# Graph layer edge loop: four PSUM banks for edge products with three pairs ahead, three banks for sums

## The chip, the cores and the metric

The kernel runs on one core of one Trainium2 chip. The metric is the device time of one execution in microseconds (us). The kernel before takes 6811.75 us, the median of three runs (6805.44 to 6826.25). The profiled execution is a fourth one, of 6786.33 us.

## The reference: what is computed

The program is a graph attention layer, a mixture of experts, a five-layer graph convolution and a second mixture, each with a residual add. The change touches the graph convolution alone. On 3125 nodes of 256 features and 53,125 edges (sorted by destination) with 128 features each, every layer `l` computes:

```
xl   = h @ W[l] + b[l]
ee   = edge_attr @ We[l] + be[l]
msg  = norm * relu(xl[row] + ee)
agg  = zeros_like(xl).at[col].add(msg)
conv = agg + relu(xl + root[l]) / deg
h    = h + (relu of, except in the last layer) batch_norm(conv)
```

All of it is in float32.

## The kernel before, in words

`graph_layers` loops over the five layers. In each, `graph_layer_inputs` makes the table `xl_table` in DRAM, `graph_layer_edges` runs the edge loop, and `graph_layer_norm` normalises. The change is in `graph_layer_edges`, with two small edits in `constants` and in `lagging_bases`.

The edges are padded to 416 tiles of 128. The edge loop has 26 iterations (`ITERS`) of 16 tiles (`BODY`), and an iteration works in eight pairs of tiles; `u` is the pair's number in its iteration, 0 to 7. So a layer has 208 pairs and the five layers have 1040. Every engine has its own instruction stream, and they meet only at semaphores. For a pair the work is:

- POOL (L1730) gathers the 128 source rows of each tile by an indirect DMA, two gathers a pair, into a buffer `g` of 16 tiles. The gather of a pair of the next iteration waits (L1745 to L1747) until DVE and ACT have used the same slots in this one.
- SP (L1705, L1708) loads the gather's indices and the edge features `ea`, in two halves of eight tiles. A half of `ea` is loaded again when its four product pairs are done (`used`, L1716).
- PE `products` (L1761) multiplies edge features by `We`, two tiles into one PSUM bank of `ep`. Two banks (`EB = 2`) are used in turn, and the wait at L1758 holds the products of a pair until DVE has read the pair two before. They are issued two pairs ahead of the sums.
- DVE `add_pair` (L1849) adds the gathered rows to the products and writes `msg`. It waits for the products, the two gathers, and the sums that last read this slot of `msg`.
- ACT (L1833) applies the relu to `msg`. DVE (L1854) makes the scaled one-hot matrix of the even tile, ACT (L1815, L1818) that of the odd tile.
- PE `sums` (L1774) multiplies messages by one-hot matrices into one PSUM bank of `ps`. Four banks are used in turn (`SB = 8` tiles), so the wait at L1769 is for the pair four before to have been added.
- DVE `add_sums` (L1862) adds a tile's sums to its window of `agg`, at an address that a register holds. It runs `LAG = 4` tiles behind, so at pair `u` DVE adds the sums of pair `u - 2`.

At pair `u` the order on PE is: products of `u + 2`, sums of `u`, and at `u = 1` also `node_tile` (L1783), the root term of one node tile. On DVE it is: `add_pair(u)`, `add_sums(u - 2)` of the even tile, the one-hot matrix, `add_sums(u - 2)` of the odd tile; at `u = 0` it also loads 16 window addresses into registers, and at `u = 6` and 7 it adds the node tile. On ACT it is: one-hot matrix of the odd tile, at `u = 3` the relu of the node tile (L1829, which waits for `node_tile`), then the relu of pair `u`.

A matmul of this source is recorded as two, so the profile has eight matmuls for the sums of a pair and four for its products.

Of the kernel before, what the change touches and what calls it, by code (L numbers as in the profile page):

```python
# [24 lines left out]
P = 128  # L25
# [14 lines left out]
GROW = HROW + HEADS  # L40
ACC = NP + P
LAG = 4
LAYERS = 5
XROW = D + 2
PARTS = 3
# [20 lines left out]
class Kernel:  # L66


    def __init__(self, nc, a, ctx):
        self.nc, self.a, self.ctx = nc, a, ctx  # L70
        self.sems, self.live = ctx.enter_context(ExitStack()), []
        sb = lambda n, s, d=F32: ctx.enter_context(nc.sbuf_tensor(n, s, d))
        dr = lambda n, s, d=F32: nc.dram_tensor(n, s, d, kind="Internal").ap()
        self.x = sb("x_res", [P, NT, D])
        self.ident = sb("ident", [P, P])
        self.iota_row = sb("iota_row", [P, P])
        self.base_row = sb("base_row", [1, ET], I32)
        self.base_lag = sb("base_lag", [1, LAG + ET], I32)
        self.block_row = sb("block_row", [1, ET], I32)
        self.dst_rel = sb("dst_rel", [P, ET])  # L80
        self.mean = sb("mean", [P, NT])
        self.rstd = sb("rstd", [P, NT])
        self.eps = sb("eps", [P, 1])
        self.agg = sb("agg", [P, K, ACC])
        self.h = sb("h", [P, K, ACC])
        self.dinv_row = sb("dinv_row", [P, ACC])
        self.floor = sb("floor", [P, LAYERS])
        self.logits = sb("logits", [P, NT, EX])
        self.weight = sb("weight", [P, 2, NT])
        self.write_row = sb("write_row", [P, 2, NT], I32)  # L90
        self.read_row = sb("read_row", [P, 2, NT], I32)
        self.group_expert = sb("group_expert", [1, 64], I32)
        self.h_table = dr("h_table", [ACC, GROW])
        self.e_rows = dr("e_rows", [ITERS, P, BODY, GROW])
        self.ea_parts = dr("ea_parts", [EA, EP], BF16)
        self.ew_parts = sb("ew_parts", [EA, D], BF16)
        self.rel_row = dr("rel_row", [1, EP], BF16)
        self.alpha_d = dr("alpha_d", [EP, HEADS])
        self.attn_d = dr("attn_d", [EP, HEADS])
        self.deg_d = dr("deg_d", [NT, P])  # L100
        self.xl_table = dr("xl_table", [NP, XROW])
        self.slots = {m.layer: m.groups * m.rows for m in FFN}
        self.x_buf = {l: dr(f"x_buf{l}", [self.slots[l], D]) for l in (0, 1)}
        self.y_buf = {l: dr(f"y_buf{l}", [self.slots[l], D]) for l in (0, 1)}
# [25 lines left out]
    return read_bases(engine, regs, k.base_row, tile)  # L130


def lagging_bases(k, engine, regs, tile):

    return read_bases(engine, regs, k.base_lag, tile)


def read_bases(engine, regs, row, at):
# [10 lines left out]
def constants(k):  # L149
    nc, a = k.nc, k.a  # L150
    ROWS = ET // 4
    with ExitStack() as c:
        sem, sb, bank = makers(k, c, "k")
        dst = sb("dst_cols", [P, ET], I32)
        basb = sb("base_bcast", [P, ET], I32)
        edge_dst, first = sb("edge_dst", [ROWS, 4, P], I32), sb("first", [ROWS, 4], I32)
        inside, block0 = sb("inside", [ROWS, 4], I32), sb("block0", [ROWS, 4], I32)
        rel = sb("rel", [ROWS, 4, P], BF16)
        loaded, made, ints, zeroed, cleared, blocks, related = (sem(n) for n in (
            "loaded", "made", "ints", "zeroed", "cleared", "blocks", "related"))  # L160
        block = c.enter_context(nc.Block())

        @block.sync
        def _(sp):
            sp.dma_start(k.base_row[:], a["dst_first"]).then_inc(loaded, 16)
            sp.dma_start(edge_dst[:], a["dst_row"].rearrange("a (p t e) -> (a p) t e", t=4, e=P)).then_inc(loaded, 16)
            sp.dma_start(first[:], a["dst_first"].rearrange("a (p t) -> (a p) t", t=4)).then_inc(loaded, 16)
            sp.dma_start(k.base_lag[:, LAG:], a["dst_first"]).then_inc(loaded, 16)
            sp.dma_start(dst[:], a["dst_cols"]).then_inc(loaded, 16)
            sp.dma_start(basb[:], a["dst_first"].broadcast_to([P, ET])).then_inc(loaded, 16)  # L170
            sp.dma_start(k.x[:], a["x"].rearrange("(t p) d -> p t d", p=P)).then_inc(loaded, 16)
            sp.wait_ge(zeroed, 1)

            sp.dma_start(k.h_table[NP:ACC, :], k.agg[:, 0, 0:GROW]).then_inc(cleared, 16)
            sp.wait_ge(related, 1)
            sp.dma_start(k.rel_row.rearrange("a (p t e) -> (a p) t e", t=4, e=P), rel[:]).then_inc(cleared, 16)
            sp.wait_ge(loaded, 112)
            sp.wait_ge(cleared, 32)

        @block.gpsimd  # L180
        def _(pool):
            nc.gpsimd.iota(k.iota_row[:], [[1, P]], base=0, channel_multiplier=0,
                           allow_small_or_imprecise_dtypes=True).then_inc(made, 1)
            nc.gpsimd.memset(k.ident[:], 0.0).then_inc(ints, 1)
            pool.wait_ge(ints, 1)
            nc.gpsimd.affine_select(out=k.ident[:], in_=k.ident[:], compare_op=ALU.not_equal, fill=1.0, base=0,
                                    pattern=[[-1, P]], channel_multiplier=1).then_inc(made, 1)

        @block.vector
        def _(dve):  # L190

            nc.vector.memset(k.agg[:], 0.0).then_inc(zeroed, 1)
            nc.vector.memset(k.eps[:], EPS).then_inc(made, 1)

            nc.vector.memset(k.h[:, :, NP:ACC], 0.0).then_inc(made, 1)
            nc.vector.memset(k.dinv_row[:, NP:ACC], 0.0).then_inc(made, 1)
            nc.vector.memset(k.base_lag[:, 0:LAG], 0).then_inc(made, 1)
            nc.vector.memset(k.floor[:, 0:LAYERS - 1], 0.0).then_inc(made, 1)
            nc.vector.memset(k.floor[:, LAYERS - 1:], -FMAX).then_inc(made, 1)
            dve.wait_ge(loaded, 112)  # L200
            nc.vector.tensor_scalar(k.block_row[:], k.base_row[:], 7, None, ALU.arith_shift_right).then_inc(made, 1)
            nc.vector.tensor_scalar(inside[:], first[:], P - 1, None, ALU.bitwise_and).then_inc(blocks, 1)
            dve.wait_ge(blocks, 1)
            nc.vector.tensor_tensor(block0[:], first[:], inside[:], ALU.subtract).then_inc(blocks, 1)
            dve.wait_ge(blocks, 2)
            nc.vector.tensor_tensor(rel[:], edge_dst[:], block0[:].unsqueeze(2).broadcast_to([ROWS, 4, P]),
                                    ALU.subtract).then_inc(related, 1)
            nc.vector.tensor_tensor(k.dst_rel[:], dst[:], basb[:], ALU.subtract).then_inc(made, 1)
# [1479 lines left out]
def graph_layer_edges(k, l):  # L1688


    nc, a, g = k.nc, k.a, k.gl
    EB, SB = 2, 8
    START_AT = BODY - LAG
    ep, ps, rp = g.banks[0:EB], g.banks[EB:EB + SB // 2], g.banks[EB + SB // 2]
    start = g.start
    block = g.open()

# [54 lines left out]
    def _(pe):  # L1752
# [12 lines left out]
        def sums(it, u):  # L1765
            pe.wait_ge(g.relu, it * (BODY // 2) + u + 1)
            pe.wait_ge(g.hot, it * (BODY // 2) + u + 1)
            pe.wait_ge(g.act_hot, it * (BODY // 2) + u + 1 + 2)
            pe.wait_ge(g.added, it * BODY + 2 * u + 2)  # L1769
            for i in range(2):  # L1770
                j = 2 * u + i
                for b in range(K):
                    at = i * D + b * P
                    last = nc.tensor.matmul(ps[u % (SB // 2)][:, at:at + P], g.msg[:, j, b * P:(b + 1) * P],  # L1774
                                            g.onehot[:, j, :], start=True, stop=True)
            last.then_inc(g.summed, 2)

# [9 lines left out]
        def body(it, final):  # L1787
            for u in range(BODY // 2):

                if u + 2 < BODY // 2:  # L1790
                    products(it, u + 2)
                elif not final:
                    products(it + 1, u + 2 - BODY // 2)
                sums(it, u)
                if u == 1:
                    node_tile(it)

        products(0, 0)
        products(0, 1)
        with pe.Fori(0, ITERS - 1) as it:  # L1800
            body(it, False)
        body(ITERS - 1, True)
# [33 lines left out]
    def _(dve):  # L1836
# [20 lines left out]
        def add_sums(n, u, i, base):  # L1857
# [1 line left out]
            dve.wait_ge(g.summed, n + 2 + BODY)  # L1859
            window = k.agg[:, :, bass.ds(base, P)]  # L1860
            dve.wait_ge(g.added, n + i + SB)
            nc.vector.tensor_tensor(window, window, ps[u % (SB // 2)][:, i * D:(i + 1) * D]  # L1862
                                    .rearrange("p (b n) -> p b n", b=K), ALU.add).then_inc(g.added, 1)

        def start_tile(it, step):
# [13 lines left out]
        def body(it, first):  # L1879
            seen = it * 16 + l * (16 * ITERS) + 16  # L1880
            for u in range(BODY // 2):
                add_pair(it, u, seen)
                if u == 0:
                    bases = lagging_bases(k, dve, base_regs, it * BODY)
                for i in range(2):
                    if 2 * u >= LAG or not first:
                        add_sums(it * BODY + 2 * u - LAG, u - LAG // 2, i, bases[2 * u + i])
# [8 lines left out]
        body(0, True)  # L1896
        with dve.Fori(1, ITERS) as it:
            body(it, False)
        for i, base in enumerate(lagging_bases(k, dve, base_regs[0:LAG], ET)):
            add_sums(ET - LAG + i // 2 * 2, (BODY - LAG + i) // 2, i % 2, base)  # L1900
        dve.wait_ge(g.added, ET + SB)

# [227 lines left out]
```

## Time and profile before

| | |
|---|---|
| runs, us | 6805.44, 6811.75, 6826.25 |
| profiled execution, us | 6786.33 |
| its span, us | 6784.7 |
| mean granted TensorE clock | 0.805 of full speed |
| PE busy | 4343.0 us, 64% |
| POOL busy | 2764.5 us, 41% |
| DVE busy | 3048.1 us, 45% |
| ACT busy | 1972.4 us, 29% |

The span runs from the first to the last instruction of the program. Shares are averages over all stages. The edge loops of the five layers lie between 2392 and 6224 us from the span's start, and only rows of that stretch bear on the change. In a row of a timeline an entry in brackets is the time that the engine was idle before the instruction, with what ended it; "remote" there means that a semaphore update ended the wait and came with no recorded instruction close before it, "issue" that no update was recorded.

### The profile page before, as it was taken

How to read it: one execution, taken by the hardware profiler on the slowest of the kernel's cores; microseconds unless marked ns; L12 is line 12 of the kernel's file. 1: busy time of each engine (PE TensorE's matmuls, PEld its weight loads, DVE VectorE, ACT ScalarE, POOL GpSimd, SP SyncE). 2: the span in 40 equal slices, each digit the busy share in tenths (PEclk: the TensorE clock that was granted, in tenths of full speed). 3: DMA queues.
4: the chain of work that ended last, by engine and by line, in shares of the span. 5: the costliest groups of instructions: out<-in, count | busy, mean ns of one | idle time of the engine just before them, and what ended most of it. 6: DMA issues, size and time to landing. Idle time of an engine off the chain costs nothing. (4 is left out here: it accounts for less than half of the span.)

```text
span 6784.7 us, 97259 instructions
## 1 busy us (share of the span) xinstructions
PE 4343.0 (64%) x21805; PEld 3583.0 (53%) x21806; DVE 3048.1 (45%) x6902; ACT 1972.4 (29%) x4303; POOL 2764.5 (41%) x3021
## 2 busy tenths in 40 slices
PE   4666643652996467775776566675676757775392
PEld 3444433542885356664666555564565646664261
DVE  4433457752001645554454544455454445555303
ACT  1111110010231034442444434442444424444120
POOL 2444422533002155553555445553555535553101
PEclk8787766975998588887888788887888878887596
DMA  4555563632453144442444344343443424442131
GB/s 137 158 160 156 159 190 95 176 91 79 184 192 127 35 125 122 116 121 87 116 123 116 88 121 114 108 118 92 116 115 109 117 87 119 121 116 72 47 108 53
DMA packets 461211, 794.76 MB, mean 117 GB/s; under 512 B 221403, under 2 KB 278412, under 8 KB 450551
## 3 DMA queue, kind: packets, MB, share of 16 engines
q0 software_dynamic: 130720, 364.17, 19.4%
q1 hardware_dynamic: 322967, 401.22, 19.0%
q10 hardware_dynamic: 7488, 28.97, 1.4%
q8 instruction: 14, 0.23, 0.0%
q14 instruction: 22, 0.18, 0.0%
HBM read 671.50 MB, written 123.52 MB: 117 GB/s over the span
## 5 line engine op out<-in xcount | busy, mean ns | idle before, releaser
L1730 POOL DMA_INDIRECT g_g<-xl_table,g_idx x2080 | 1968.0, 946 | 1663.3 <-issue 1146.3
L1774 PE MATMUL g_b<-g_onehot,g_msg 128*128 128x128 f32 x8320 | 1375.9, 319 | 893.3 <-DVE agg L1862 336.4
L1774 PEld LDWEIGHTS g_b<-g_onehot,g_msg 128*128 128x128 f32 x8320 | 1296.6, 229 | 1109.8 <-DVE agg L1862 796.8
L1862 DVE TENSOR_TENSOR agg<-agg,g_b 128x256 f32 x2080 | 868.0, 417 | 1331.8 <-remote 854.0
L1761 PE MATMUL g_b<-g_we,g_ea 128*128 128x256 f32 x4160 | 1291.4, 441 | 185.9 <-DVE g_msg L1849 92.4
L1761 PEld LDWEIGHTS g_b<-g_we,g_ea 128*128 128x128 f32 x4160 | 844.8, 225 | 302.0 <-DVE g_msg L1849 112.9
L1833 ACT ACTIVATE g_msg<-g_msg 128x512 f32<-128x512 f32 x1040 | 650.8, 626 | 1124.5 <-DVE g_msg L1849 1002.7
L1849 DVE TENSOR_TENSOR g_msg<-g_g,g_b 128x512 f32<-128x512 f32 x1040 | 710.4, 683 | 483.4 <-remote 222.2
L544 PE MATMUL sc_pe_h<-ae_h_rows,sc_onehot 128*128 x1664 | 506.9, 456 | 218.5 <-DVE sc_prod L616 152.4
L512 POOL DMA_INDIRECT sc_g<-h_table,sc_idx x416 | 399.5, 960 | 452.9 <-DVE sc_alpha L608 330.0
L544 PEld LDWEIGHTS sc_pe_h<-ae_h_rows,sc_onehot 128*128 128x128 f32 x1664 | 348.4, 220 | 332.1 <-issue 272.7
L1818 ACT ACTIVATE g_onehot<-g_away,g_g 128x128 f32<-128x128 f32 x1040 | 513.0, 493 | 34.6
L1815 ACT ACTIVATE g_away<-iota_row,dst_rel 128x128 f32<-128x128 f32 x1040 | 404.9, 389 | 245.6 <-DMA g_g<-xl_table,g_idx 229.1
L616 DVE TENSOR_TENSOR sc_prod<-sc_enc,sc_pe_h 128x528 f32<-128x528 f32 x208 | 146.1, 702 | 513.2 <-remote 324.7
L1854 DVE TENSOR_SCALAR g_onehot<-iota_row,dst_rel,g_g 128x128 f32<-128x128 f32 x1040 | 363.7, 350 | 4.2 <-issue 4.2
L1392 DVE TENSOR_TENSOR ex_y<-ex_yp,ex_b 128x256 f32<-128x256 f32 x96 | 40.8, 425 | 716.5 <-PE ex_yp L1346 716.5
L1335 PE MATMUL ex_hp<-ex_xt,ex_w 128*128 128x256 f32 (+1 forms) x1280 | 343.1, 427 | 11.4 <-DMA ex_b<-in_f_b 11.4
L1346 PE MATMUL ex_yp<-ex_w,ex_hid 128*128 128x256 f32 x1536 | 342.0, 382 | 7.6 <-ACT ex_hid L1372 7.5
L895 PE MATMUL at_ps<-at_onehot,at_msg 128*128 128x128 f32 x1664 | 238.4, 300 | 160.2 <-DVE at_msg L832 91.9
L577 ACT ACTIVATE sc_enc<-sc_pe_e 128x512 f32<-128x512 f32 x208 | 120.8, 597 | 747.1 <-PE sc_pe_e L533 464.5
L1407 POOL DMA_DIRECT2D y_buf<-ex_y x40 | 29.0, 726 | 714.2 <-DVE ex_y L1392 714.2
L1346 PEld LDWEIGHTS ex_yp<-ex_w,ex_hid 128*128 128x128 f32 x1536 | 288.5, 190 | 55.1 <-issue 14.4
(256 smaller groups left out, 3536.0 us busy)
## 6 DMA issues: line engine op xcount, KB each, us to landing
g_ea<-in_ea SPq DMA_DIRECT2D x260, 512.0 KB
ex_w<-in_f_w SPq DMA_DIRECT2D x80, 1024.0 KB, 7.4
e_rows<-sc_g SPq DMA_DIRECT2D x208, 272.0 KB
g_g<-xl_table,g_idx POOLq DMA_INDIRECT x2080
at_g<-e_rows ACTq DMA_DIRECT2D x52, 544.0 KB, 4.0
at_g<-e_rows SPq DMA_DIRECT2D x52, 544.0 KB, 3.7
xl_table<-g_rows SPq DMA_DIRECT2D x25, 640.0 KB, 4.0
sc_rel<-rel_row SPq DMA_DIRECT2D x52, 256.0 KB
```

The lines of the kernel that those rows point to most:

```text
L512: nc.gpsimd.indirect_dma_start(out=g[:, j, :], out_offset=None, in_=k.h_table[:, :], in_offset=bass.IndirectOffsetOnAxis(ap=idx[:, q, j % ...
L544: last = nc.tensor.matmul(pe_h[u % HB][:, i, 0:HROW], onehot[:, q, b, (at + i) * P:(at + i + 1) * P], k.h_rows[:, bass.ds(blocks[2 * u + i ...
L1346: last = nc.tensor.matmul(yp[b % 2][:, 0:D], hid[:, m, b * P:(b + 1) * P], w2[:, s, m * D:(m + 1) * D], start=(m == 0), stop=(m == M - 1))
L1730: nc.gpsimd.indirect_dma_start(out=g.g[:, j, :], out_offset=None, in_=k.xl_table[:, :], in_offset=bass.IndirectOffsetOnAxis(ap=g.idx[:, q, ...
L1761: last = nc.tensor.matmul(ep[u % EB][:, i * D:(i + 1) * D], g.ea[:, q, (at + i) * P:(at + i + 1) * P], g.we[:], start=True, stop=True)
L1774: last = nc.tensor.matmul(ps[u % (SB // 2)][:, at:at + P], g.msg[:, j, b * P:(b + 1) * P], g.onehot[:, j, :], start=True, stop=True)
L1815: nc.scalar.activation(g.away[:, j // 2 % 2, :], k.iota_row[:], ACT.Abs, bias=k.dst_rel[:, bass.ds(it * BODY + j, 1)], scale=-1.0).then_in ...
L1818: nc.scalar.activation(g.onehot[:, j, :], g.away[:, j // 2 % 2, :], ACT.Relu, bias=g.g[:, j, D:D + 1], scale=g.g[:, j, D + 1:XROW]).then_i ...
L1833: nc.scalar.activation(m, m, ACT.Relu).then_inc(g.relu, 1)
L1849: nc.vector.tensor_tensor(g.msg[:, 2 * u:2 * u + 2, :], g.g[:, 2 * u:2 * u + 2, 0:D], ep[u % EB][:, 0:2 * D].rearrange("p (a d) -> p a d", ...
L1854: nc.vector.tensor_scalar(g.onehot[:, j, :], k.iota_row[:], k.dst_rel[:, bass.ds(it * BODY + j, 1)], g.g[:, j, D:D + 1], ALU.is_equal, ALU ...
L1862: nc.vector.tensor_tensor(window, window, ps[u % (SB // 2)][:, i * D:(i + 1) * D] .rearrange("p (b n) -> p b n", b=K), ALU.add).then_inc(g ...
```

## The change

`EB` goes from 2 to 4 banks for products and `SB` from 8 to 6 tiles, that is from 4 to 3 banks for sums. With the bank of the node tile, all eight are in use now, where one was free. Products are issued three pairs ahead of the sums instead of two, with one more pair ahead of the loop; their wait for DVE is now for the pair four before. Eight pairs don't divide by three banks, so a table `BANK3` says which bank a pair's sums use, and `FREE3` how many pairs back its last user lies: three, but two at `u = 4` and 5. The lag of `add_sums` stays at four tiles; its row of addresses gets two more zeros in front (`PRE = 6`) and is read two further on, which gives the same addresses.

```diff
+PRE = 6
-def lagging_bases(k, engine, regs, tile):
+def lagging_bases(k, engine, regs, tile, lag=LAG):
-    return read_bases(engine, regs, k.base_lag, tile)
+    return read_bases(engine, regs, k.base_lag, tile + PRE - lag)
...
-    EB, SB = 2, 8
+    EB, SB, LAG = 4, 6, 4
+    BANK3 = [0, 1, 2, 0, 2, 0, 1, 2]
+    FREE3 = [3, 3, 3, 3, 2, 2, 3, 3]
...
-            pe.wait_ge(g.added, it * BODY + 2 * u + 2)
+            pe.wait_ge(g.added, it * BODY + 2 * u + 2 + SB - 2 * FREE3[u])
...
-                    last = nc.tensor.matmul(ps[u % (SB // 2)][:, at:at + P], g.msg[:, j, b * P:(b + 1) * P],
+                    last = nc.tensor.matmul(ps[BANK3[u]][:, at:at + P], g.msg[:, j, b * P:(b + 1) * P],
...
-                if u + 2 < BODY // 2:
-                    products(it, u + 2)
+                if u + 3 < BODY // 2:
+                    products(it, u + 3)
                 elif not final:
-                    products(it + 1, u + 2 - BODY // 2)
+                    products(it + 1, u + 3 - BODY // 2)
                 sums(it, u)
...
         products(0, 1)
+        products(0, 2)
...
-            nc.vector.tensor_tensor(window, window, ps[u % (SB // 2)][:, i * D:(i + 1) * D]
+            nc.vector.tensor_tensor(window, window, ps[BANK3[u]][:, i * D:(i + 1) * D]
```

## Rows read from the trace of the kernel before

**Rows 1.** Windows of the five edge loops, summed: us, then busy us by engine.
```profile
sum 3554.00, PE 2507.96 PEld 2177.43 DVE 1748.96 ACT 1527.26 POOL 1968.04; mean PE 501.59 PEld 435.49 DVE 349.79 ACT 305.45 POOL 393.61
```
**Rows 2.** Timeline of DVE: one-hot matrix of pair 0, iterations 1 and 25, first and third layer.
```profile
2442.39 0.34 DVE L1854 TENSOR_SCALAR g_onehot<-iota_row,dst_rel,g_g 128x128 f32<-128x128 f32 x1
3076.94 0.34 DVE L1854 TENSOR_SCALAR g_onehot<-iota_row,dst_rel,g_g 128x128 f32<-128x128 f32 x1
...
3980.28 0.34 DVE L1854 TENSOR_SCALAR g_onehot<-iota_row,dst_rel,g_g 128x128 f32<-128x128 f32 x1
4642.77 0.34 DVE L1854 TENSOR_SCALAR g_onehot<-iota_row,dst_rel,g_g 128x128 f32<-128x128 f32 x1
```
**Rows 3.** Timeline of DVE in a short iteration, from its pair 0 to the next.
```profile
3529.63 0.34 DVE L1854 TENSOR_SCALAR g_onehot<-iota_row,dst_rel,g_g 128x128 f32<-128x128 f32 x1
...
3539.55 0.42 DVE L1862 TENSOR_TENSOR agg<-agg,g_b 128x256 f32 x1 [5.17 <-remote]
...
3541.66 0.42 DVE L1862 TENSOR_TENSOR agg<-agg,g_b 128x256 f32 x1
...
3549.03 0.42 DVE L1862 TENSOR_TENSOR agg<-agg,g_b 128x256 f32 x1 [4.84 <-remote]
...
3555.59 0.34 DVE L1854 TENSOR_SCALAR g_onehot<-iota_row,dst_rel,g_g 128x128 f32<-128x128 f32 x1
```
**Rows 4.** Timeline of PE in the same short iteration: the sums of pair 4.
```profile
3542.67 1.05 PE L1774 MATMUL g_b<-g_onehot,g_msg 128*128 128x128 f32 x8
```
**Rows 5.** Timeline of DVE in a long iteration, from its pair 0 to the next.
```profile
4199.25 0.34 DVE L1854 TENSOR_SCALAR g_onehot<-iota_row,dst_rel,g_g 128x128 f32<-128x128 f32 x1
...
4211.97 0.69 DVE L1849 TENSOR_TENSOR g_msg<-g_g,g_b 128x512 f32<-128x512 f32 x1 [7.48 <-remote]
...
4213.16 0.41 DVE L1862 TENSOR_TENSOR agg<-agg,g_b 128x256 f32 x1
...
4215.47 0.42 DVE L1862 TENSOR_TENSOR agg<-agg,g_b 128x256 f32 x1 [1.30 <-PE g_b L1774]
...
4217.08 0.69 DVE L1849 TENSOR_TENSOR g_msg<-g_g,g_b 128x512 f32<-128x512 f32 x1 [0.60 <-PE g_b L1761]
4218.88 0.42 DVE L1862 TENSOR_TENSOR agg<-agg,g_b 128x256 f32 x1 [1.11 <-issue]
...
4228.40 0.34 DVE L1854 TENSOR_SCALAR g_onehot<-iota_row,dst_rel,g_g 128x128 f32<-128x128 f32 x1
```
**Rows 6.** Timeline of PE in the same long iteration.
```profile
4203.43 1.03 PE L1761 MATMUL g_b<-g_we,g_ea 128*128 128x256 f32 x4
4204.30 1.05 PE L1774 MATMUL g_b<-g_onehot,g_msg 128*128 128x128 f32 x8
...
4213.27 2.07 PE L1774 MATMUL g_b<-g_onehot,g_msg 128*128 128x128 f32 x8 [7.05 <-ACT g_msg L1833]
...
4216.83 1.92 PE L1774 MATMUL g_b<-g_onehot,g_msg 128*128 128x128 f32 x8
```
**Rows 7.** Timeline of POOL in the same long iteration.
```profile
4209.16 0.94 POOL L1730 DMA_INDIRECT g_g<-xl_table,g_idx  x1 [0.30 <-issue]
4214.83 0.94 POOL L1730 DMA_INDIRECT g_g<-xl_table,g_idx  x1 [4.73 <-DVE g_msg L1849]
```
**Rows 8.** Timeline of ACT in the same long iteration.
```profile
4213.46 0.49 ACT L1818 ACTIVATE g_onehot<-g_away,g_g 128x128 f32<-128x128 f32 x1
```
**Rows 9.** DVE's `add_pair` (L1849): what ended its waits, us and times.
```profile
  remote: 222.2, 41
  PE g_b L1761: 65.5, 121
```
**Rows 10.** Products (L1761): DVE's `add_pair` as what ended PE's waits, us and times.
```profile
  DVE g_msg L1849: 205.3, 153
```
**Rows 11.** The products as a group: busy us, mean ns of one, idle before.
```profile
L1761 PE MATMUL g_b<-g_we,g_ea 128*128 128x256 f32 x4160 | 1291.4, 441 | 185.9 <-DVE g_msg L1849 92.4
```
**Rows 12.** Gather issues (L1730): duration in ns, least, median, most.
```profile
L1730 POOL DMA_INDIRECT g_g<-xl_table,g_idx x2080: 940/946/1049, 2393.5 to 6208.4; - x190
```

More of the change, by code:

```diff
@@ L77, in __init__ @@
         self.base_row = sb("base_row", [1, ET], I32)
-        self.base_lag = sb("base_lag", [1, LAG + ET], I32)
+        self.base_lag = sb("base_lag", [1, PRE + ET], I32)
         self.block_row = sb("block_row", [1, ET], I32)
@@ L167, in _ @@
             sp.dma_start(first[:], a["dst_first"].rearrange("a (p t) -> (a p) t", t=4)).then_inc(loaded, 16)
-            sp.dma_start(k.base_lag[:, LAG:], a["dst_first"]).then_inc(loaded, 16)
+            sp.dma_start(k.base_lag[:, PRE:], a["dst_first"]).then_inc(loaded, 16)
             sp.dma_start(dst[:], a["dst_cols"]).then_inc(loaded, 16)
@@ L196, in _ @@
             nc.vector.memset(k.dinv_row[:, NP:ACC], 0.0).then_inc(made, 1)
-            nc.vector.memset(k.base_lag[:, 0:LAG], 0).then_inc(made, 1)
+            nc.vector.memset(k.base_lag[:, 0:PRE], 0).then_inc(made, 1)
             nc.vector.memset(k.floor[:, 0:LAYERS - 1], 0.0).then_inc(made, 1)
@@ L1883, in body @@
                 if u == 0:
-                    bases = lagging_bases(k, dve, base_regs, it * BODY)
+                    bases = lagging_bases(k, dve, base_regs, it * BODY, LAG)
                 for i in range(2):
@@ L1898, in _ @@
             body(it, False)
-        for i, base in enumerate(lagging_bases(k, dve, base_regs[0:LAG], ET)):
+        for i, base in enumerate(lagging_bases(k, dve, base_regs[0:LAG], ET, LAG)):
             add_sums(ET - LAG + i // 2 * 2, (BODY - LAG + i) // 2, i % 2, base)
```

## Prediction, made before the kernel ran

> **What bounds the kernel now.** I read the windows of the five edge loops first. They take 3554 us, and no engine fills them: PE is busy for 2508 us, POOL for 1968, DVE for 1749, ACT for 1527 [rows 1]. POOL needs more than its busy time. Its gathers stand 0.30 us apart at the closest [rows 7], and one takes 946 ns [rows 12]: 1.25 us a gather, 20 us for the 16 of an iteration.
>
> Next I timed the iterations, from one one-hot matrix of pair 0 to the next. The 24 iterations between the marks take 634.55 us in the first layer, 26.4 each, and 662.49 us in the third, 27.6 each [rows 2]. There are two kinds, a short one of 25.96 us [rows 3] and a long one of 29.15 us [rows 5]; 24 short ones would take 623, so the first layer has an excess of 11.5 us over short ones, the third 39.5.
>
> What fills an iteration is seen in DVE's timeline. In the short one DVE stops twice for some 5 us, before an `add_sums`, until a "remote" update [rows 3]. The long one shows what that is. PE records the products of pair 4 at 4203.43 and the sums of pair 2 at 4204.30, each over in about 1 us [rows 6]; but `add_pair(4)`, which waits for those products, starts at 4211.97, after 7.48 us of idle time [rows 5]. PE's work was done; its semaphore updates came late. Meanwhile POOL worked off its gathers, the last one issued from 4209.16 to 4210.10 [rows 7], and the release came 1.9 us after it. Then PE goes on, at the lower of its two clock levels, for the eight matmuls of one pair take 2.07 and 1.92 us there against 1.05 before [rows 6]. So the loop runs in bursts: the late PE updates stop DVE, POOL drains and idles for 4.73 us [rows 7], and all start again. What ends last in a burst is the wait of `add_sums` for sums: at 4215.47 for those of pair 3, which began at 4213.27 and took 2.07, and at 4218.88 for those of pair 4, from 4216.83 and 1.92 long [rows 5, 6].
>
> **The change part by part.** *Products a pair earlier, with four banks.* Two waits go. PE's products no longer wait for DVE: 205.3 us over 153 waits [rows 10], 0.2 us a pair. DVE's `add_pair` no longer waits for a product just made: 65.5 us over 121 waits, and 222.2 over 41 for a late update [rows 9]. What is late next?
>
> Take the long iteration. Its products of pair 4 now stand ahead of the sums of pair 1 and were seen in time. `add_pair(4)` (0.69 us) then runs at once; the next in DVE's stream is `add_sums(2)`, and the sums of pair 2 come after those products on PE, so their update is late as well. DVE stops there until about 4211.9 as before. After the release its one-hot matrix is 0.6 us earlier, but POOL's gather at 4214.83 also waits for ACT's one-hot matrix, which ends at 13.46 + 0.49 = 4213.95 [rows 8], later than DVE's, and ACT was held by the node tile. `add_sums(3)` at 4215.47 waits for the same sums as before. The 0.60 us before `add_pair(6)` goes, and becomes part of the 1.11 before `add_sums(4)` [rows 5]. So 0.69 + 0.60 us are freed and both end in a wait for sums. In the short iteration both long stops are already before `add_sums` [rows 3].
>
> The wait that PE loses goes the same way: it must still wait for the relu and the one-hot matrices of pair `u` before the sums, and it does as much work between two sums as ever, one product pair. I take 0 for both. The bounds: all of DVE's 65.5 us and 41 times 0.69 = 28 on the path give 94 us less; the most that can be lost is a rival's, below.
>
> *Three banks for sums.* Six of eight pairs wait for the adds of `u - 3`. DVE issues those one step before the one-hot matrix of pair `u`, for which PE waits anyway, so they cost 0. At `u = 4` and 5 the wait is for `u - 2`. In the long iteration the second add of pair 2 ends at 4213.16 + 0.41 = 4213.57 and the sums of pair 4 start at 4216.83 [rows 5, 6], 3.3 us of margin; in the short one it ends at 3542.08 and they start at 3542.67 [rows 3, 4], 0.6 us. I take 0, and note that the margin in the short one is thin.
>
> *A third product pair ahead of each loop.* It takes 4 matmuls of 441 ns [rows 11], 1.8 us at most a layer and 9 in all, while PE has no messages to sum. I take 0 (bounds 0 and +9). Two more zeros in a row of addresses are once in a kernel, nothing beside 20 us.
>
> *SP's stream.* The features of a half are loaded once four product pairs are done, which is now one pair earlier against the sums. Nothing is added to any queue: SP still has two index loads and two feature loads an iteration. The shift changes which transfer runs beside which gathers. Its cost can't be read off; it is bounded by iterations changing their kind, in the rivals.
>
> The sum is 0, to which I add -4 us for the first iterations of the layers and for the few waits of `add_pair` that no later one takes up (about 5% of the 94). Against the profiled 6786.33 us that gives 6782; the median of the runs is 25 us above the profiled execution, so 6808 in their terms.
>
> A rule of the Trainium skill speaks against denser DVE work. By "SBUF — State Buffer", section "Who interferes with whom", a DVE `tensor_scalar` can enter a mode that takes the port pair shared with GpSimd, which then cannot write the descriptors of its own DMAs. If each of the 1040 one-hot matrices of 0.34 us held up a gather's issue, that would be 354 us. The trace does not show it: 2080 issues take 940 to 1049 ns [rows 12], though the two engines run side by side all along.
>
> **The rivals.**
> 1. *Long iterations become short, faster.* The long one is marked by DVE stopping at `add_pair(4)` for a late product, and exactly that wait is gone. If the pattern then falls into the short one, the excess of 11.5 to 39.5 us a layer goes, in five layers 58 to 198, about 128: 6684. Against it: the release and the POOL backlog are the same wherever DVE stands.
> 2. *Short iterations become long, slower.* The earlier feature load runs beside other gathers, PE's updates are late at another point, and the burst before it is worked off with a larger backlog. One more pair in the backlog is 2.5 us of POOL. It decides when a short iteration's stop moves from `add_sums(1)` past the sums of pair 1. If all were long: 24 times 29.15 = 700 us, 37 more than the third layer has and 65 more than the first, in five layers 185 to 325, about 255: 7067. If the other layers only become like the third, at most 4 times 28 = 112 more: 6924.
> 3. *Three banks bind, slower.* If PE catches up with DVE in the short iteration, the sums of pairs 4 and 5 wait for one more add of 0.42 us each: 2 times 0.42 times 130 iterations = 109 us: 6921. It decides once the 0.6 us margin is used up, and PE's lost wait of 0.2 us a pair eats into it.
> 4. *The freed waits count in full, faster.* The 94 us of the bounds: 6718. For it speaks that they are in DVE's stream; against it the waits for sums right behind.
>
> **How the numbers follow.** A change of under 0.3% (20 us) is about what a measurement of this kernel can't tell from none. My forecast (waits move, time stays) has 0.46; its own range is 6780 to 6835, of which 0.36 lies within 0.3%, 0.06 is faster and 0.04 slower. Rival 1 has 0.24, rival 4 has 0.08, both faster. Rival 2 has 0.16 (its part to 6924 the likelier), rival 3 has 0.06, both slower. So faster 0.38, same 0.36, slower 0.26. The range reaches from rival 1 nearly with its upper bound, 6650, to the milder form of rivals 2 and 3, 6925.
>
> **What would show each step right or wrong.** In the profile after, `add_pair` should hardly wait for PE any more, "remote" or not, and the products' waits for `add_pair` (205.3 us) should be gone, while the waits before `add_sums` and those of PE before the sums grow by about as much. Iterations should still take 26.0 or 29.2 us. Gathers should still take 0.946 us. A wait of PE for `add_sums` that ends right with the second add at `u = 4` and 5 would show rival 3. Iterations of a third length, or a different share of long ones, would show that the lateness of PE's updates depends on what I held fixed, and then the time may lie anywhere in the range.

## The result and the profile after

The changed kernel takes 7246.07 us, the median of four runs (7239.81 to 7266.57), beside 6819.0 for the kernel before in four runs (6805.44 to 6837.1): a ratio of 1.063 (1.0595 to 1.0666), 427 us slower. The prediction was 6808 in a range of 6650 to 6925; the time lies above it. The profiled execution took 7239.81 us, with a mean TensorE clock of 0.779 of full speed against 0.805 before.

First the head of the page: the span, and busy time, share and instructions of each engine.

```profile
span 7238.2 us, 97634 instructions
PE 4499.6 (62%) x21805; PEld 3733.2 (52%) x21806; DVE 3051.8 (42%) x6902; ACT 1978.4 (27%) x4303; POOL 2800.9 (39%) x3021
```

DVE's busy time is what it was (3051.8 against 3048.1 us). The windows of the five edge loops answer to [rows 1]:

```profile
sum 3972.00, PE 2612.94 PEld 2281.13 DVE 1787.83 ACT 1532.21 POOL 1977.63; mean PE 522.59 PEld 456.23 DVE 357.57 ACT 306.44 POOL 395.53
```

No engine has more to do: each has as many instructions as before. PE's busy time in the loops grows by 105 us at the lower mean clock; the rest of the loss is idle time. From the first gather to the last `add_sums` the five loops take 3940.4 us against 3569.8 (+371). The span is 453.5 us longer, so 83 us lie outside the loops, and the first and last instruction of each stage show 67 of them in `attention_sums`, which the diff does not touch: 351.9 us before, 418.5 after (the other 16 are in `edge_scores`, whose code and addresses are unchanged; a later run of banks and order alone has 20 there). It reads its window addresses by the same `lagging_bases`. That is the lead.

DVE's timeline of one iteration after, from the last `add_pair` of the one before to the next one-hot matrix of pair 0, answers to [rows 3, 5]:

```profile
4350.60 0.69 DVE L1853 TENSOR_TENSOR g_msg<-g_g,g_b 128x512 f32<-128x512 f32 x1 [0.83 <-PE g_b L1777]
4355.02 0.42 DVE L1866 TENSOR_TENSOR agg<-agg,g_b 128x256 f32 x1 [3.73 <-issue]
4355.36 0.34 DVE L1858 TENSOR_SCALAR g_onehot<-iota_row,dst_rel,g_g 128x128 f32<-128x128 f32 x1
...
4363.75 0.42 DVE L1866 TENSOR_TENSOR agg<-agg,g_b 128x256 f32 x1 [3.90 <-PE g_b L1777]
...
4368.21 0.42 DVE L1866 TENSOR_TENSOR agg<-agg,g_b 128x256 f32 x1 [2.85 <-remote]
...
4371.89 0.42 DVE L1866 TENSOR_TENSOR agg<-agg,g_b 128x256 f32 x1 [0.55 <-PE g_b L1777]
...
4378.33 0.42 DVE L1866 TENSOR_TENSOR agg<-agg,g_b 128x256 f32 x1 [4.50 <-remote]
...
4385.19 0.42 DVE L1866 TENSOR_TENSOR agg<-agg,g_b 128x256 f32 x1 [3.72 <-issue]
4385.53 0.34 DVE L1858 TENSOR_SCALAR g_onehot<-iota_row,dst_rel,g_g 128x128 f32<-128x128 f32 x1
```

It takes 30.2 us. At pair 0 DVE stands for 3.73 us between `add_pair(0)` and the first `add_sums`, with "issue" as the reason: no update was waited for. The same place before:

```profile
4083.57 0.69 DVE L1849 TENSOR_TENSOR g_msg<-g_g,g_b 128x512 f32<-128x512 f32 x1 [0.83 <-issue]
4085.49 0.42 DVE L1862 TENSOR_TENSOR agg<-agg,g_b 128x256 f32 x1 [1.24 <-issue]
```

Between these two instructions DVE's sequencer loads 16 addresses into registers. It is not counted as busy, so it shows in no table of engines; the view of its source line has it (count, duration in ns as least, median and most, first and last start). After, and then before:

```profile
L140 DVEq TENSOR_LOAD <-base_lag x162: 965/3608/3851, 1118.1 to 6678.4; - x162
```

```profile
L139 DVEq TENSOR_LOAD <-base_lag x162: 349/1100/1345, 1103.5 to 6224.6; - x162
```

The load takes 3.61 us where it took 1.10; all 162 take 556.4 us against 174.2, summed over the trace. 135 are in the graph loops (27 a layer) and 27 in `attention_sums`. The addresses are the same numbers, but with `PRE = 6` each read starts two 4-byte elements, 8 bytes, further on in the row. Boundaries are counted here from the row's start.

What else the profile after shows are the moved waits. `add_pair` answers to [rows 9], the products to [rows 10]: what ended the waits, us and times.

```profile
  DMA g_g<-xl_table,g_idx: 55.8, 5
  PE g_b L1777: 52.9, 64
  DVE agg L1879: 42.4, 53
  issue: 4.1, 5
  remote: 2.5, 3
```

```profile
  DMA g_ea<-in_ea: 93.9, 10
  issue: 71.1, 36
```

In the groups (count, then busy us and mean ns, then idle before), the products answer to [rows 11] and the gathers to [rows 12]; `add_sums` was idle for 1331.8 us before.

```profile
L1733 POOL DMA_INDIRECT g_g<-xl_table,g_idx x2080 | 1978.2, 951 | 2002.6 <-issue 921.9
...
L1866 DVE TENSOR_TENSOR agg<-agg,g_b 128x256 f32 x2080 | 868.9, 418 | 2014.1 <-remote 1095.2
L1764 PE MATMUL g_b<-g_we,g_ea 128*128 128x256 f32 x4160 | 1322.7, 450 | 81.8 <-DMA g_ea<-in_ea 45.9
```

### The profile page after: what moved, and what is told of

Its sections match the earlier page's. It is cut to its first block and busy times, and to the rows that moved or that the text cites. A ratio compares the mean times of both kernels' runs of the same rounds, so it can differ in the third digit from the quotient of the medians.

```text
span 7238.2 us, 97634 instructions
## 1 busy us (share of the span) xinstructions
PE 4499.6 (62%) x21805; PEld 3733.2 (52%) x21806; DVE 3051.8 (42%) x6902; ACT 1978.4 (27%) x4303; POOL 2800.9 (39%) x3021
## 5 line engine op out<-in xcount | busy, mean ns | idle before, releaser
L1777 PE MATMUL g_b<-g_onehot,g_msg 128*128 128x128 f32 x8320 | 1454.9, 331 | 1264.5 <-DVE agg L1866 882.5
L1777 PEld LDWEIGHTS g_b<-g_onehot,g_msg 128*128 128x128 f32 x8320 | 1372.0, 241 | 1502.0 <-DVE agg L1866 738.4
L1866 DVE TENSOR_TENSOR agg<-agg,g_b 128x256 f32 x2080 | 868.9, 418 | 2014.1 <-remote 1095.2
L1764 PE MATMUL g_b<-g_we,g_ea 128*128 128x256 f32 x4160 | 1322.7, 450 | 81.8 <-DMA g_ea<-in_ea 45.9
L1764 PEld LDWEIGHTS g_b<-g_we,g_ea 128*128 128x128 f32 x4160 | 874.5, 233 | 177.1 <-DMA g_ea<-in_ea 48.0
L545 PE MATMUL sc_pe_h<-ae_h_rows,sc_onehot 128*128 x1664 | 528.0, 470 | 231.8 <-DVE sc_prod L617 203.4
L896 PE MATMUL at_ps<-at_onehot,at_msg 128*128 128x128 f32 x1664 | 270.7, 330 | 194.0 <-DVE at_msg L833 113.5
L896 PEld LDWEIGHTS at_ps<-at_onehot,at_msg 128*128 128x128 f32 x1664 | 250.9, 238 | 213.6 <-DVE agg L919 125.4
L833 POOL TENSOR_TENSOR at_msg<-at_g,at_attn 128x256 f32<-128x256 f32 x312 | 214.5, 721 | 352.3 <-DMA at_attn<-attn_d 181.8
```

What stands on the lines that cost most here:

```text
L545: last = nc.tensor.matmul(pe_h[u % HB][:, i, 0:HROW], onehot[:, q, b, (at + i) * P:(at + i + 1) * P], k.h_rows[:, bass.ds(blocks[2 * u + i ...
L896: last = nc.tensor.matmul(ps[u][:, at:at + P], msg[:, j, b * P:(b + 1) * P], onehot[:, j, :], start=True, stop=True)
L1764: last = nc.tensor.matmul(ep[u % EB][:, i * D:(i + 1) * D], g.ea[:, q, (at + i) * P:(at + i + 1) * P], g.we[:], start=True, stop=True)
L1777: last = nc.tensor.matmul(ps[BANK3[u]][:, at:at + P], g.msg[:, j, b * P:(b + 1) * P], g.onehot[:, j, :], start=True, stop=True)
L1866: nc.vector.tensor_tensor(window, window, ps[BANK3[u]][:, i * D:(i + 1) * D] .rearrange("p (b n) -> p b n", b=K), ALU.add).then_inc(g.adde ...
```

## The experiments

The theory: the register loads cost the time ("address theory"). The rival: the banks and the order of issue cost it, by moving the bursts (rival 2 of the prediction) or by the waits for three banks (rival 3).

One thing has to be known to read the numbers. The kernel before took 6809 and 6822 us in two of the groups of runs, as in the profile above, and 5569 to 5578 in the others, on other chips. Each experiment is compared with the kernel before in its own group. I call the two the slow and the quick condition. In the quick one the gathers follow each other 0.30 us apart. The trace shows what differs. In a quick run (three banks for sums alone, below) all 1040 semaphore updates of the sums are recorded within 0.1 us of the last matmul's end. In the slow condition, in the kernel before, 382 are; 360 are recorded later, 2.1 us on the median, and for the others no update of their own is recorded. No update of ACT's relu is recorded late there (232 of 1040 are not recorded). The stages without gathers don't differ (`attention_sums` takes 352 us in both); the loops take 3569.8 against 2647.3 us, and `edge_scores`, which gathers too, 870 against 582. What makes a chip show the one or the other is not settled; the only chip on record for two groups was quick in both.

**The row of addresses alone** (run twice). The kernel before, with only the longer row:

```diff
+PRE = 6
...
-        self.base_lag = sb("base_lag", [1, LAG + ET], I32)
+        self.base_lag = sb("base_lag", [1, PRE + ET], I32)
...
-    return read_bases(engine, regs, k.base_lag, tile)
+    return read_bases(engine, regs, k.base_lag, tile + PRE - LAG)
```

> The kernel before with one edit of the change alone: two more zeros in front of the address row (PRE = 6), so that DVE's load of 16 registers starts 8 bytes further on. Theory A, the load's address: each load takes 3.6 us instead of 1.1, 2.5 us on DVE's path in 135 loads of the graph loops and 27 of the attention sums, some 380 us in all: 7200 (7150 to 7250), iterations of the graph loop 2.5 us longer. Rival B, banks and product order: the row is nothing, 6819 and loads of 1.1 us.

Measured: 5692.52 against 5569.4 us, 1.0222 (1.0205 to 1.0239). Its loads, and DVE's first `add_sums` of an iteration:

```profile
L140 DVEq TENSOR_LOAD <-base_lag x162: 966/3609/3861, 814.9 to 5133.8; - x162
```

```profile
3410.28 0.42 DVE L1863 TENSOR_TENSOR agg<-agg,g_b 128x256 f32 x1 [3.74 <-issue]
```

Both rows are those of the changed kernel, so the row of addresses alone makes them. `attention_sums` takes 418 us for 352, which leaves 57 of the 123 us for the loops. Their 135 loads grow by 329 us there, so most of it is hidden: the gathers set the pace in this condition, at some 20 us an iteration, and DVE has time to spare. The expectation's 7200 was for the slow condition.

> The kernel before with the row of the change alone (PRE = 6), with all gathers, for the condition in which the kernel before takes some 6815 us (its first run was where it takes 5569). Theory A: nearly all of the 427 us of the change, at least the 382 us of the longer loads: 7200 to 7250. Rival: well under 7150, and banks and order make up the rest.

Measured: 5698.61 against 5578.24, 1.0216 (1.0199 to 1.0234).

**The changed kernel in the same condition.**

> The changed kernel itself, beside the others. The first four experiments ran where the kernel before takes 5569 us, not 6819, so the change's own cost there is not known yet. Theory A, the load's address alone: where the kernel before takes 5569 it costs what the row alone cost (123 us), 5692; where it takes 6819 it costs 427 again. Rival B, banks and order add to it: 20 us or more above the row alone.

Measured: 5694.83 against 5568.99, 1.0222 (1.0205 to 1.0239). The whole change costs here what its row of addresses costs.

**Banks and order without the longer row** (run four times, in three groups of the quick condition and one of the slow one).

```diff
-PRE = 6
+PRE = 4
```

> The changed kernel with the row as before (PRE = 4): four product banks, products three pairs ahead, three banks for sums, and loads that start where they did. Theory A: loads of 1.1 us again, and what is left is what the banks and the order do; 7246 less 382 gives 6864, my forecast for these parts was 6808 (6780 to 6835). Rival B: about 7200, loads of 3.6 us or not.

Measured: 5568.63 against 5569.4, 1.0001 (0.9992 to 1.0011). The loads take 1.10 us again. Repeated:

> The changed kernel with the row as before (PE's banks and product order alone), again, for the case that this group runs where the kernel before takes 6819. Theory A: 6864 there (7246 less the 382 us of the loads), 5569 where the kernel before takes 5569, as in its first run. Rival B: over 7000.

Measured: 0.9999 (0.9989 to 1.0009).

> The changed kernel with the row as before, with all gathers, in that condition. With half of the gathers left out these parts cost 25 us. Theory A: 6815 to 6865. Rival: over 6900, the bursts with late PE updates get longer through the order.

Measured: 1.0000 (0.999 to 1.0009). That group was quick too, which left the slow condition untested. POOL's timeline of this run shows why nothing else counts in the quick one, and its `add_pair` waits for gathers:

```profile
3409.84 0.95 POOL L1733 DMA_INDIRECT g_g<-xl_table,g_idx  x1 [0.30 <-DVE g_onehot L1858]
3411.09 0.94 POOL L1733 DMA_INDIRECT g_g<-xl_table,g_idx  x1 [0.30 <-issue]
3412.34 0.94 POOL L1733 DMA_INDIRECT g_g<-xl_table,g_idx  x1 [0.30 <-issue]
```

```profile
  DMA g_g<-xl_table,g_idx: 517.8, 578
```

One gather starts each 1.25 us, 16 of them take 20 us, and an iteration takes 20.10.

**Which offset is slow.** The kernel before with 20 and with 8 elements in front, so that the reads start 64 and 16 bytes further on:

```diff
+PRE = 20
```

> The kernel before with 16 more zeros in front of the row (PRE = 20), loads 64 bytes further on. If a load is slow because it starts off a 64-byte or smaller boundary: loads of 1.1 us, 6819. If any shift or a longer row is slow: 3.6 us, about 7200.

```diff
+PRE = 8
```

> The kernel before with four more zeros in front of the row (PRE = 8), loads 16 bytes further on. If the boundary that counts is 16 bytes or less: 1.1 us a load, 6819. If it is 32 or 64 bytes: loads of 3.6 us and about 7200.

Measured: 5572.83 us, 1.0004 (0.9995 to 1.0014), and 5579.31, 1.0013 (1.0004 to 1.0023). Their loads, 20 first:

```profile
L140 DVEq TENSOR_LOAD <-base_lag x162: 349/1100/1348, 823.8 to 5023.4; - x162
```

```profile
L140 DVEq TENSOR_LOAD <-base_lag x162: 349/1102/1343, 818.7 to 5021.9; - x162
```

A longer row costs 0.1% at most by itself, and a start at a multiple of 16 bytes is enough. 8 bytes past one is slow. Other offsets were not tried.

**Can the load be hidden?** First four loads of four registers each, at the ends of pairs, instead of one of 16:

```diff
+                    if u % 2 == 1:
+                        m = (2 * u + 2) % BODY
+                        fetch_bases(k, dve, base_regs[m:m + 4], it * BODY + 2 * u + 2)
...
-                    bases = lagging_bases(k, dve, base_regs, it * BODY)
```

> The kernel before with DVE's load of 16 registers, in the attention sums and in the graph loops, cut into four loads of four registers, each issued after a pair's work and a step ahead of its use, at 16-byte boundaries. Theory A (the load stands on DVE's path where DVE sets the pace): the attention sums get 1.1 us shorter in each of 26 iterations, 29 us less; the graph loops gain nothing where POOL's gathers set the pace (20.0 us an iteration), and up to 1.2 us in 130 iterations, 156 us, where late PE updates do. So 5540 beside 5569, or 6640 to 6790 beside 6819. Rival: a load costs the sequencer as much in four pieces and nothing is gained, or the time rises.

Measured: 5591.36 against 5568.99 us, 1.0036 (1.0022 to 1.005), 22 us slower where 29 less were expected. In this form the idea falls: a load of four registers takes 0.34 us, and 624 of them 215 us together where 162 took 174; `attention_sums` went from 351 to 362 us.

```profile
L140 DVEq TENSOR_LOAD <-base_lag x624: 339/344/592, 830.5 to 5034.3; - x156
```

Then two loads of eight, each issued behind the 0.7 us of `add_pair(1)` and `add_pair(5)`, two or more pairs ahead of its use:

```diff
+                if u in (1, 5):
+                    m = (2 * u + 6) % BODY
+                    fetch_bases(k, dve, base_regs[m:m + 8], it * BODY + 2 * u + 6)
...
-                    bases = lagging_bases(k, dve, base_regs, it * BODY)
```

> The kernel before with DVE's load of 16 registers cut into two of eight, each issued right behind a DVE instruction of 0.7 us (weigh in the attention sums, add_pair in the graph loop) and two to three pairs ahead of its use. e6 had four pieces of 0.34 us at the ends of pairs and lost 20 us. Theory: the sequencer loads while the engine works, so the 1.24 us of idle time before the first add goes: 29 us less in the attention sums, and up to 160 in the graph loops where POOL doesn't set the pace. 6630 to 6790 beside 6815, 5540 beside 5569. Rival: the sequencer has no lead over the engine, the load costs what it did, and nothing is gained.

Measured: 5571.71 against 5578.24 us, 0.9988 (0.9978 to 0.9997), 6.5 us less. It is the only version whose interval lies below 1, but the gain is small beside the 29 us that were expected; `attention_sums` takes 342 us for 351. It was not run in the slow condition.

```profile
L140 DVEq TENSOR_LOAD <-base_lag x318: 594/598/841, 823.2 to 5007.1; - x159
```

**Doubling the load.** An aligned load, done twice:

```diff
+    engine.load(regs, k.base_lag[0:1, bass.ds(tile, len(regs))])
```

> The kernel before with the aligned load of 16 registers done twice: 1.1 us more for each of 162 loads, 178 us in all on DVE's sequencer. Theory A: DVE has some 2 us of slack an iteration in the graph loops where POOL sets the pace, so only the 27 loads of the attention sums count, 29 us: 5598 beside 5569. Where PE's updates are late it has none, and all counts: 6819 plus 178, 6997. Rival (the address matters by something else than the load's duration): no change.

Measured: 5569.7, 0.9999 (0.999 to 1.0009), where 5598 was expected. The trace has 162 loads of 1.10 us and not 324, so the load wasn't doubled on the chip, and the run says nothing on either theory.

**Three banks for sums alone, in the quick condition** (two product banks and two pairs ahead, as before):

```diff
+    BANK3 = [0, 1, 2, 0, 2, 0, 1, 2]
+    FREE3 = [3, 3, 3, 3, 2, 2, 3, 3]
...
+            pe.wait_ge(g.added, it * BODY + 2 * u + 2 + SB - 2 * FREE3[u])
```

> The kernel before with three banks for sums alone, all gathers. With half of the gathers left out this cost 23 us. Theory: 6815 to 6860 where the kernel before takes 6815; 5569 where POOL sets the pace.

> The kernel before with three banks for sums alone (two product banks, two pairs ahead, the row as before), all gathers, for the condition in which the kernel before takes some 6820 us and banks and order together cost 111. Theory S (the banks for sums cost it, as with half of the gathers, where they alone cost 23 of 25): 6930. Theory P (the product order costs it: PE does a product pair between the late sums and DVE): 6820, at most 25 more. Where the kernel before takes 5569 to 5578 it says nothing new.

Measured: 0.9998 (0.9988 to 1.0008) and 0.9997 (0.9987 to 1.0006). The second was meant for the slow condition and met the quick one.

**Half of the gathers.** To take POOL off the path, these kernels gather only the even tile of each pair and use its rows for the odd one as well, so their messages for odd tiles are not the reference's. They ran beside a kernel before of 6809.12 us, so in the slow condition.

```diff
-            for j in (2 * u, 2 * u + 1):
+            for j in (2 * u,):
```

> Leaves out half of the graph loops' gathers: one gather a pair, and the odd tile of a pair uses the rows of the even one, so the messages of odd tiles are not the reference's; instructions of PE, DVE and ACT keep their shapes. POOL then needs 10 us an iteration instead of 20 and can't set the pace. The kernel before otherwise. Theory A: the chain of DVE and PE sets it, 20.5 us less the 2.5 us of the slow load, 18.0 an iteration: 5569 less 130 times 2.0, 5310. Rival: the loop stays at 20 us, so something else than POOL set it.

Measured: 5495.34 us, 0.8076. Of DVE's waits for a "remote" update, 1076.2 us in the kernel before, 30.1 are left, and an iteration takes 17.0 us (18.0 was expected, in the quick condition). With the banks and the order, with the row of 6, and with three banks for sums alone:

> As e9_half_gather (half of the gathers left out), with the change's four product banks, three pairs ahead and three banks for sums, the row as before. This is where PE's order can show. My prediction's step (freed product waits end up in waits for sums): the same time as e9 within 20 us. Rival 4 of the prediction (they count in full): 90 us or more below e9. Rival 3 (three banks bind): up to 109 us above e9.

> As e9_half_gather (half of the gathers left out), with the row of the change (PRE = 6, loads 8 bytes further on) and nothing else of it. Theory A: with POOL out of the way all of the 2.5 us counts in each of 135 loads of the graph loops, and in 27 of the attention sums: 382 us above e9. If DVE has slack of its own there, less.

> As e9_half_gather (half of the gathers left out), with three banks for sums alone; two product banks and two pairs ahead as before. Theory of the prediction: the waits at pairs 4 and 5 are met anyway, same as e9 within 20 us. Rival 3: 2 times 0.42 us in 130 iterations, up to 109 us above e9.

Measured: 5519.9 (+25 us beside the first), 5979.48 (+484) and 5518.22 (+23). Of the 25 us three banks for sums alone make 23; both are just above the 20 us that were to count as no change. The row costs more than its loads do and more than the 382 us expected: the loads of the loops grow by 329 us (473.8 against 144.9), and the loops by 420 (`attention_sums` by 67). PE's timeline after a load in the kernel with the row shows part of the rest:

```profile
3831.95 1.05 PE L1762 MATMUL g_b<-g_we,g_ea 128*128 128x256 f32 x4
3836.43 1.45 PE L1775 MATMUL g_b<-g_onehot,g_msg 128*128 128x128 f32 x8 [3.43 <-DVE agg L1862]
3837.67 1.91 PE L1762 MATMUL g_b<-g_we,g_ea 128*128 128x256 f32 x4
3839.37 1.62 PE L1775 MATMUL g_b<-g_onehot,g_msg 128*128 128x128 f32 x8
```

After 3.43 us without work the four product matmuls take 1.91 us for 1.05: PE runs at the lower of its two levels (1.2 against 2.4 GHz) until about 3841, when four take 1.03 us again. The mean granted clock is 0.824 there and 0.858 in the first of the four.

**Banks and order in the slow condition.** The same kernel as above with `PRE = 4`:

> The changed kernel with the row as before, all gathers, once more, for the condition in which the kernel before takes some 6815 us. Theory A (the load's address is the whole cause, the 45 us over its durations are its knock-on): 6815, or up to 25 us more as with half of the gathers. Rival (the 45 us are the order's): 6860. Second rival: over 6900. Where the kernel before takes 5569 to 5578 it says nothing new: the same time.

Measured: 6932.66 us beside 6822.05, 1.0153 (1.0104 to 1.0202), +111 us (71 to 138): slower, if less sharply measured than the rest. It is what the expectation's second rival gave (over 6900). Its loads take 1.10 us, so this is none of the address theory's. From the view of `add_pair`:

```profile
  PE g_b L1777: 71.9, 87
...
  remote: 0.8, 1
```

DVE's timeline in one iteration, and PE's and POOL's beside it:

```profile
4160.08 0.42 DVE L1866 TENSOR_TENSOR agg<-agg,g_b 128x256 f32 x1 [3.85 <-PE g_b L1777]
...
4164.53 0.42 DVE L1866 TENSOR_TENSOR agg<-agg,g_b 128x256 f32 x1 [2.85 <-remote]
...
4169.19 0.42 DVE L1866 TENSOR_TENSOR agg<-agg,g_b 128x256 f32 x1 [1.53 <-PE g_b L1777]
...
4174.66 0.42 DVE L1866 TENSOR_TENSOR agg<-agg,g_b 128x256 f32 x1 [3.54 <-remote]
```

```profile
4163.57 2.07 PE L1777 MATMUL g_b<-g_onehot,g_msg 128*128 128x128 f32 x8 [3.22 <-ACT g_msg L1837]
4165.43 1.91 PE L1764 MATMUL g_b<-g_we,g_ea 128*128 128x256 f32 x4
4167.14 1.91 PE L1777 MATMUL g_b<-g_onehot,g_msg 128*128 128x128 f32 x8
...
4169.89 1.05 PE L1777 MATMUL g_b<-g_onehot,g_msg 128*128 128x128 f32 x8
...
4175.69 1.74 PE L1777 MATMUL g_b<-g_onehot,g_msg 128*128 128x128 f32 x8 [2.12 <-DVE agg L1866]
```

```profile
4161.55 0.94 POOL L1733 DMA_INDIRECT g_g<-xl_table,g_idx  x1 [1.45 <-issue]
...
4166.00 0.94 POOL L1733 DMA_INDIRECT g_g<-xl_table,g_idx  x1 [2.26 <-ACT g_onehot L1822]
...
4176.13 0.98 POOL L1733 DMA_INDIRECT g_g<-xl_table,g_idx  x1 [2.94 <-issue]
```

DVE stops four times in the iteration, each time before `add_sums`. After 3.22 us without work PE starts again at the lower level, as in [rows 6]: eight matmuls take 2.07 us, and the granted clock is 0.50 of full speed from 4163.6 to 4168.5 and 1.00 from 4170 on. DVE's third stop, of 1.53 us, is a wait for these slow sums; after 2.12 us without work the eight take 1.74. POOL pauses three times. Between the marks of [rows 2] an iteration takes 28.15 us on the mean against 27.06, and POOL is idle beyond its 0.30 us a gather for 8.13 us of it against 7.09. That says only that POOL's own work stayed the same; it does not tell what holds it.

Do the three banks themselves hold PE? I took, for each pair from the second iteration on, the end of the last of its one-hot matrices and its relu, and the end of the second add that its bank waits for. That add was the last of them for 175 pairs, all at `u = 4` and 5, by 52 us in all. But mostly PE was still at the products issued before: with their end counted too, the add was last for 14 pairs, by 4.3 us. So rival 3's 109 us are not there: the wait as such costs under 5 us. With half of the gathers and three banks for sums alone the same count gives 1.6 us, though that kernel is 23 us slower. PE's idle time before sums, from the second iteration on, lies elsewhere than before: 483 us at pair 3, 149 at pair 6, 95 at pair 7 and 87 at pair 0 in the kernel before; 552, 17, 240 and 261 here. Stops have moved to the end and the start of the iteration.

## Why the prediction was wrong

**The step that failed** is "Two more zeros in a row of addresses are once in a kernel, nothing beside 20 us". I priced the writing of the zeros, and not the reads: 162 loads from that row, each now 8 bytes past a 16-byte boundary, and all but the six of four registers 2.51 us longer. It sits in DVE's stream between `add_pair(0)` and `add_sums`, and the one-hot matrix that PE waits for stands behind it: PE's idle time before the sums of pair 0 goes from 87 us to 534. In the quick condition the row explains the whole loss (1.0222 alone and 1.0222 with the rest). In the slow one it is an estimate, the difference of 427 and 111, some 316 us; alone with all gathers it was not run there. The parts of the profiled executions agree: between the kernel with `PRE = 4` (3698.7 us of loops) and the changed one (3940.4) lie 242 us, and 67 in `attention_sums`, 309 together. The loads in the loops take 461.0 us against 140.6, 320 more, so some 80 us of them lie beside waits that were there anyway. Neither a rival nor the range had this.

**Freed waits move to the sums: right; at no cost: wrong.** The products' 205.3 us of waits for `add_pair` [rows 10] are gone, and `add_pair`'s 65.5 for products and 222.2 for a late update [rows 9] are down to 2.5. The 52.9 us that are left to PE's account are another wait, the sums that last read its slot of `msg`. All of it turned up before `add_sums`, as forecast (1331.8 us idle before, 2014.1 after, the longer loads in it). But the sum was not 0, and this is the second step that failed. With the loads as before the change still costs 111 us in the slow condition, at 6932.66 us. That is the milder form of rival 2 (6924), held at a part of its 0.16. Its sign in the trace is there: the loops of the five layers took 700.6, 706.3, 726.5, 727.8 and 708.5 us, and take 739.7, 740.3, 737.8, 744.2 and 736.8 with banks and order alone, all a little above the longest. I held that DVE stops "as before" and read this off one iteration; the pattern of stops changed instead. Why the stops fall where they do is not shown. The "two kinds" of iteration were read off two examples. Of the 120 between the marks, 60 lie within half a microsecond of 26 us and 23 of 29, and 37 between; with banks and order alone 104 lie at 28 or 29.

**Three banks: 0, right as to the wait** (4.3 us). `FREE3` gives three at `u = 6` too, where the bank's last user lies five pairs back; the pair that it names has been waited for at `u = 5` already, so it adds no wait. Whether they have a share in the 111 us by shifting the pattern stays open; with half of the gathers they made 23 of 25 us, with all gathers they were not run alone in the slow condition.

**The third product pair ahead, SP's stream: taken as 0, not shown.** Neither was tried by itself, and a share in the 111 us is open for both.

**Iterations "still 26.0 or 29.2 us": wrong.** They take some 30 us in the changed kernel, where the longer load has a part in it; with banks and order alone it is the share of long ones that changed. In the prediction's words that shows that the lateness of the updates depends on what it held fixed.

**Gathers still 0.946 us: right.** They take 0.951, so the rule on DVE's port that the prediction names shows no price in these rows either.

Of the register load one page gives a price: the Trainium skill, "Runtime: NRT & Kernel Launch", section "Instruction fetch mechanics", says that a register load costs about 200 ns a register even in bulk. The page speaks of registers loaded from HBM ahead of a kernel, and this load reads a row in SBUF. Here only the load off the boundary comes near that figure: 3.61 us for 16 registers is 226 ns each, while the load at the boundary takes 1.10 us, 69 ns each. The measurement decides.

## What to carry to other kernels

Whoever moves data in a row from which an engine loads registers has to price every load from it, not the edit: keep the start of each at a multiple of 16 bytes from where a fast load starts, and look at the sequencer's own instructions (here `TENSOR_LOAD`) when an idle time is put down to "issue". A stage that the diff doesn't touch and that still gets slower points at what the two share. In a loop whose engines stop and start in bursts, waits that move can't be summed from one iteration; bound them by the slowest pattern that the trace shows.

## What the runs showed of the hardware

- DVE's load of 16 registers from a row in SBUF takes 1.10 us at multiples of 16 bytes from the row's start (0, 16 and 64) and 3.61 us 8 bytes past one; one of four takes 0.35 and 0.97 (the least column of both kernels, the load behind each loop), one of eight at a boundary 0.60.
- The same kernel took 6809 to 6822 us on some chips and 5569 to 5578 on others. In the slow condition PE's updates come late in the stages that gather (382 of the sums' 1040 recorded within 0.1 us), in the quick one none of the sums' does. With half of the gathers 755 of 1040 come in time. The banks and the order cost 111 us in the one and nothing measurable in the other, so a result got on one chip need not hold on the next.
- PE's idle time costs twice: after 3.22 us without work eight matmuls take 2.07 us for 1.05, at a granted clock of 0.50 for 1.00; after 2.12 us they take 1.74.
